# Linear attention in a fused block: chunks of 128 tokens become chunks of 64, two side by side on the partitions

## The reference, cut to what matters

```python
Q, K, V = xn @ WQ.T + bQ, xn @ WK.T + bK, xn @ WV.T + bV      # 16 heads of 64
gate = silu(xn @ Wg.T + bg)
alpha = sigmoid(alpha_logit)                                  # one decay per head and state row
def step(h, qkv):                                             # scanned over the 2048 tokens
    q, k, v = qkv
    h = alpha[None, :, :, None] * h + k[:, :, :, None] * v[:, :, None, :]
    return h, einsum('bhi,bhij->bhj', q, h)
y = (o * gate) @ WO.T + bO
x = layernorm(x + residual + y)
x = layernorm(x + coupling_network(x))
```

## Time and profile before

| | |
|---|---|
| three runs | 1981.52, 1983.5, 1986.42 us; median 1983.5 |
| the profiled execution | 1980.89 us, of which the span is 1979.2 us |
| PE busy | 1853.6 us, 94% |
| PE weight loads | 1409.0 us, 71% |
| DVE, ACT, POOL busy | 1087.8, 749.1, 315.3 us (55%, 38%, 16%) |
| granted clock | 0.983 of full over the span |

### The profile page before, as it was taken

One profiled execution on the slowest core, in us unless ns is written; L12 is line 12 of the kernel. 1 busy time (PEld: TensorE's weight loads), 2 busy tenths in 40 slices (PEclk: granted clock), 3 DMA queues, 4 the chain that ended last, 5 costly groups with the idle time before them and its releaser, 6 DMA issues.

```text
span 1979.2 us, 46951 instructions
## 1 busy us (share of the span) xinstructions
PE 1853.6 (94%) x19178; PEld 1409.0 (71%) x19178; DVE 1087.8 (55%) x2230; ACT 749.1 (38%) x1326; POOL 315.3 (16%) x246
## 2 busy tenths in 40 slices
PE   5999999999799999999889999999979999999996
PEld 4888787853587878784368787878338888888732
DVE  7646464545754655554665555555375554545546
ACT  3424242434342424334443333333444333334344
POOL 3111111101211111210221212021022121111002
PEclk9999999999899999999989999999999999999998
DMA  4000000000100000000010000000001000000001
GB/s 153 2 13 2 12 2 12 2 1 1 54 2 13 2 12 2 12 2 0 0 55 2 13 2 13 2 13 1 0 19 37 2 13 2 12 2 13 1 0 43
DMA packets 23342, 26.86 MB, mean 14 GB/s; under 512 B 3185, under 2 KB 22001, under 8 KB 23153
## 3 DMA queue, kind: packets, MB, share of 16 engines
q1 hardware_dynamic: 21152, 19.62, 3.1%
q10 hardware_dynamic: 2000, 4.20, 0.6%
HBM read 15.42 MB, written 8.39 MB: 12 GB/s over the span
## 4 chain that ended last, share of the span: by engine, by line
PE 83%; DVE 7%; issue 6%; ACT 4%; DMA 0%; POOL 0%; DVEq 0%; ACTq 0%; SPq 0%
PE bank L803 37%; PE bank L875 11%; PE bank L1029 7%; PE bank L830 6%; PE bank L866 6%; PE bank L857 5%; PE bank L847 3%; PE bank L839 2%; DVE v_sb L771 2%; DVE x_nf L764 2%; PE bank L1072 1%; DVE cpl L760 1%; PE bank L794 1%; ACT q_sb L415 1%; PE bank L1046 1%
## 5 line engine op out<-in xcount | busy, mean ns | idle before, releaser
L415 ACT ACTIVATE q_sb<-q_sb,pows 128x384 f32<-128x384 f32 (+2 forms) x387 | 168.7, 498 | 469.4 <-DVE q_sb L599 469.4
L721 DVE TENSOR_TENSOR o_g<-bank,gate 128x512 f32<-128x512 f32 x128 | 88.6, 692 | 443.1 <-PE bank L866 443.1
L345 POOL TENSOR_TENSOR k_end<-k_sc,pows 128x512 f32<-128x512 f32 x129 | 135.8, 1053 | 833.8 <-DVE k_sc L590 833.8
L433 ACT ACTIVATE h_bd<-h_seq,pows 64x256 f32<-64x256 f32 x256 | 130.0, 508 | 313.9 <-DVE h_seq L699 310.6
L875 PE MATMUL bank<-wo,o_g 128*128 128x256 f32 x1024 | 226.2, 379 | 0.0
L875 PEld LDWEIGHTS bank<-wo,o_g 128*128 128x128 f32 x1024 | 193.2, 190 | 26.2
L683 DVE COPY_PREDICATED att<-causal,bank 128x1024 f32<-128x1024 int32 x128 | 167.8, 1311 | 8.2 <-PE bank L830 8.2
L675 DVE TENSOR_TENSOR v_sb<-bank,bias_v 128x512 f32<-128x512 f32 x128 | 88.3, 692 | 103.8 <-PE bank L803 101.3
L857 PEld LDWEIGHTS bank<-q_sb,h_bd 128*128 128x128 f32 x1024 | 134.0, 191 | 11.3
L866 PE MATMUL bank<-att,v_sb 128*64 128x128 f32 x2048 | 140.1, 279 | 0.0
L830 PE MATMUL bank<-q_sb,k_sc 64*32 64x128 f32 (+3 forms) x8192 | 137.0, 237 | 0.0
(11 more groups left out here) (137 smaller groups left out, 3365.3 us busy)
## 6 DMA issues: line engine op xcount, KB each, us to landing
x_in<-in_x SPq DMA_DIRECT2D x17, 512.0 KB, 3.5
out_y<-o_g SPq DMA_DIRECT2D x16, 512.0 KB, 2.9
v_sb<-in_wq ACTq DMA_DIRECT2D x1, 1024.0 KB, 5.2
v_sb<-in_wk SPq DMA_DIRECT2D x1, 1024.0 KB, 8.3
o_g<-in_wg ACTq DMA_DIRECT2D x1, 1024.0 KB, 10.6
o_g<-in_wv ACTq DMA_DIRECT2D x1, 1024.0 KB, 13.4
wo<-in_wo ACTq DMA_DIRECT2D x1, 1024.0 KB, 17.1
bias_v<-in_bV SPq DMA_DIRECT2D x1, 512.0 KB, 9.7
```

What stands on the lines that cost most here:

```text
L345: nc.gpsimd.tensor_tensor(k_end[:].rearrange("p (a z) (b r) -> p a (z b) r", z=2, r=BL), k_sc[:].rearrange("p (a z) (b r) -> p a (z b) r", ...
L415: last = nc.scalar.activation(q_sb[:, p % 2, d].rearrange("p (a z) n -> p a (z n)", z=2)[:, :, reach], q_sb[:, p % 2, 0].rearrange("p (a z ...
L433: nc.scalar.activation(h_bd[rows, :, e * DH:(e + 1) * DH], h_seq[rows, :, :], ACT.Copy, scale=pows[rows, p, HP:HP + 1]).then_inc(s_hbd, 1)
```

## The change

The change makes chunks of `SC` = 64 tokens. The 128 partitions of a token group now hold two chunks, `r` = 0 and 1, on partitions 0 to 63 and 64 to 127; there are 8 chunks (`NSC`) in a stage in place of 4.

- `from_state`: 16 products on 64x64 places (head `e` uses rows 64e.. and columns 64e..) with 64 columns, from a plain `h_dec`, in place of 4 products of 128x128 with 128 columns from the block-diagonal `h_bd`. The output goes to banks 5 and 6, one per `r`.
- `from_chunk`: 16 products on 64x64 places with 64 columns, in place of 8 on 128x64 with 128 columns.
- `updates`: 16 products on 64x64 places in place of 8 on 128x64, 64 columns each. They go to the upper halves of banks 2 and 3, whose lower halves have the scores.
- `scores`: still 32 products per pair, but of 2 and 1 query blocks (64 and 32 columns).
- DVE: 8 dependent state steps instead of 4; they wait for scores and update both. `masked` covers 512 elements per partition in place of 1024, always behind the steps. The copy of `h_st` moves from DVE to POOL. The gating reads two banks.
- ACT: one shifted query copy instead of three, and one decay of 128x512 instead of two of 64x256.
- PE waits for its own `from_state` before `from_chunk`. In the last pair, the second `y_part` goes behind `from_state`.
- The start makes seven fewer table entries of decay powers and clears no `h_bd`.

The diff, cut to its core:

```diff
+R = 2
+SC = C // R
+SB = SC // BL
+NSC = NC * R
...
+        def update_of(c, r, rows):
+            return bank[2 + r][rows, NC * SC + c * DH:NC * SC + (c + 1) * DH]
...
@@ gpsimd
+            def state_carried(b, p, n):
+                pool.wait_ge(s_h0, b + 1)
+                pool.wait_ge(s_hend, n + C0)
+                pool.wait_ge(s_hdec, n + C0)
+                pool.sem_inc(s_passed_pool, 1)
+                nc.gpsimd.tensor_copy(h_seq[:, 0, :], h_st[:, p, :]).then_inc(s_hs, 1)
...
                     for p in range(NP - 1):
+                        state_carried(b, p, it * NP + p)
                         ends_of(p + 1, it * NP + p + 1)
...
@@ scalar
-                for d in range(1, NB):
+                for d in range(1, SB):
...
-                for e in range(2):
-                    rows = slice(e * DH, (e + 1) * DH)
-                    nc.scalar.activation(h_bd[rows, :, e * DH:(e + 1) * DH], h_seq[rows, :, :],
-                                         ACT.Copy, scale=pows[rows, p, HP:HP + 1]).then_inc(s_hbd, 1)
+                nc.scalar.activation(h_dec[:], h_seq[:], ACT.Copy, scale=pows[:, p, HP:HP + 1]).then_inc(s_hdec, 1)
...
@@ vector
-                        dve.wait_ge(s_hbd, n * 2 + C0)
-                        nc.vector.tensor_copy(h_seq[:, 0, :], h_st[:, p, :]).then_inc(s_hs, 1)
                         dve.wait_ge(s_upd, n + 1 + C0)
-                        for c in range(NC):
-                            dve.wait_ge(s_hs, n * NC + c + 1 + C0)
+                        dve.wait_ge(s_score, n + 1 + C0)
+                        for j in range(NSC):
+                            dve.wait_ge(s_hs, n * NSC + j + 1 + C0)
...
@@ tensor, scores
                 for c in range(NC):
-                    for g in range(NB):
-                        count = g + 1 if c % 2 else NB - g
+                    for g in ((1, 3, 0, 2) if c % 2 else (0, 2, 1, 3)):
+                        chunk, place = g // SB, g % SB
+                        count = place + 1 if c % 2 else SB - place
...
@@ tensor, updates
                 for c in range(NC):
-                    for e in range(2):
-                        h = 2 * p + e
-                        last = nc.tensor.matmul(
-                            bank[6][e * DH:(e + 1) * DH, c * DH:(c + 1) * DH],
-                            k_tok[:, c, e * DH:(e + 1) * DH], v_sb[:, c, h * DH:(h + 1) * DH],
-                            start=True, stop=True)
+                    for r in range(R):
+                        tok = slice(r * SC, (r + 1) * SC)
+                        for e in range(2):
+                            h = 2 * p + e
+                            last = nc.tensor.matmul(
+                                update_of(c, r, slice(e * DH, (e + 1) * DH)),
+                                k_tok[tok, c, e * DH:(e + 1) * DH], v_sb[tok, c, h * DH:(h + 1) * DH],
+                                start=True, stop=True)
...
@@ tensor, from_state
+                for r in range(R):
+                    for c in range(NC):
+                        for e in range(2):
+                            rows = slice(e * DH, (e + 1) * DH)
+                            last = nc.tensor.matmul(
+                                bank[5 + r][rows, c * SC:(c + 1) * SC], h_dec[rows, c * R + r, :],
+                                query_blocks(rows, p, c, r * SB, SB),
+                                start=(c == 0), stop=False, skip_group_check=True)
...
@@ tensor, the pair's ring
-                        pe.wait_ge(s_hbd, (n + 1) * 2 + C0)
+                        pe.wait_ge(s_hdec, n + 1 + C0)
                         pe.wait_ge(s_og, n + C0)
-                        from_state(p)
+                        pe.sem_inc(s_passed_pe, 1)
+                        from_state(p).then_inc(s_fs, 1)
...
                         pe.wait_ge(s_att, n + 1 + C0)
+                        pe.wait_ge(s_fs, n + 1)
+                        pe.sem_inc(s_passed_pe, 1)
                         from_chunk(p).then_inc(s_o, 1)
                         if p + 1 < NP:
                             pe.wait_ge(s_ktok, n + 2 + C0)
                             pe.wait_ge(s_hend, n + 1 + C0)
+                            pe.wait_ge(s_att, n + 1 + C0)
+                            pe.sem_inc(s_passed_pe, 1)
                             updates(p + 1).then_inc(s_upd, 1)
```

More of the change, by code:

```diff
@@ L127, in build, with query_blocks @@
         bank = [psum[:, n, :] for n in range(8)]
-        def query_blocks(rows, p, c, first, count):
+        def query_blocks(rows, p, c, place, count):
             view = q_sb[rows, p % 2]
-            step = -(NC * C) + BL if c % 2 else NC * C + BL
+            plane = NC * C
+            step, shifted = (BL - plane, count - 1) if c % 2 else (BL + plane, 0)
+            first = shifted * plane + c * C + place * BL
             return bass.AP(view.tensor, view.offset + first, [list(view.ap[0]), [step, count], [1, BL]])
+        def update_of(c, r, rows):
+            return bank[2 + r][rows, NC * SC + c * DH:NC * SC + (c + 1) * DH]
         def part(n, k):
@@ L830, in scores @@
                             last = nc.tensor.matmul(
[L831 to L833 removed]
+                                bank[2 + e][g * BL:(g + 1) * BL, cols], k_sc[rows, c, g * BL:(g + 1) * BL],
+                                query_blocks(rows, p, c, chunk * SB + first, count), start=True, stop=True)
                 return last
@@ L851, in updates @@
                 return last
             def from_state(p):
-                for c in range(NC):
-                    first = (NB - 1) * NC * C + c * C if c % 2 else c * C
-                    nc.tensor.matmul(bank[5][:, c * C:(c + 1) * C], h_bd[:, c, :],
-                                     query_blocks(slice(0, P), p, c, first, NB),
-                                     start=(c == 0), stop=False, skip_group_check=True)
+                for r in range(R):
[6 more added lines that the diff above has]
+                                start=(c == 0), stop=False, skip_group_check=True)
```

133 lines of the change are left out of this document (66 added, 67 removed).

## The result

The changed kernel takes 2022.1 us (median of 4 runs, 2018.5 to 2025.9), the kernel before 1982.7 (4 runs, 1981.5 to 1986.4): a ratio of 1.0196 [1.0177, 1.0215]. That it is slower is clear; whether by a little more or a little less than 2% is not. I had said 1977, range 1942 to 2016. The profiled execution has a span of 2016.8 us against 1979.2 before: 37.6 us to explain. First the page of the changed kernel, for the earlier trace rows: busy times, the queue that brings the program, the chain.

The account below looks back on a forecast made before the run. PE, busy 94% of the span, was taken to bound the kernel. Rings +1, last pairs -3, first pairs' scores -2 and start -1.5 made -5.5 us: 1980.9 to 1975.4, stated as 1977 for the median, range 1942 to 2016.

Parts of the forecast that it names:

- the sum of a ring: PE from one `from_state` to the next, 8.20 us before: 0.26 - 0.12 + 0 - 0.13 = +0.01 us, x112 = +1 us.
- The supply of products is the bound: Rival, chance 0.17: update and scores on PE cost 0.031 us a product, ring +0.27 us, total 2007 or 2010 us.
- `from_state`, +0.26: PE's state products: 16 rounds of 0.059 us plus tile-shape changes in and out, 1.15 us against 0.89.
- Transposes to update, -0.12: PE from key transposes to update: `from_chunk` halves to 0.47 us, but waiting for `k_tok` leaves only -0.12 us per pair.
- Update, 0: PE's update products: again 8 rounds, so no change from 0.56 us; bounds -0.05 and +0.15.
- Scores, -0.13: PE's 32 score products per pair: first half scales with columns to 0.19 us, second nearly stays; 0.87 against 1.00.
- Last pair, -0.18: Last pair of each stage, no update behind it, gets all of `from_chunk`'s gain: 1.83 us against 2.01, x16 = -3 us.
- DVE becomes the bound: Rival, chance 0.16: DVE's chain of steps, mask and keys reaches 8.45 us, making PE wait; total 2005 or 2007 us.
- What is hidden: DVE's chain from scores to next keys takes 7.97 us against PE's 8.21, so its four more steps cost nothing, 0.24 spare.
- Start, -1.5: Kernel start: dropping 7 table steps of 0.20 us each saves 1.5 us.
- the first pairs' scores, -0.13: Scores of each stage's first pair, outside the ring: -0.13 us x 16 = -2 us.
- the floor of 25 ns a record: Skill's start-to-start minimum for small matmuls on PE; by it the ring would be 0.3 us more; trace's 16 ns preferred.

Follow-up runs that it names:

- the shifts of the program: Changed kernel with 64 extra semaphore increments a stage in PE's program, 1999.6 us; the same with 16 increments a stage, 2006.4 us.
- the block-diagonal run: Changed kernel with `from_state` back to 8 full-array products of 64 columns from block-diagonal states: 2145.5 us, ratio 1.0813 to the kernel before.

## Why the prediction was wrong

The step that failed is the sum of a ring and its "there are 112 such rings": it takes the small products' rounds as all that their number costs. Nothing in it asks whether the instructions themselves come in time. What the runs showed in its place: PE stops about once a stage in the scores until a packet of its program is there, 19.2 us in all, and longer at each stage's head, 11.6 us with the slow clock behind it.

- **What was missing.** The stops in the scores, 19.2 us, and the longer and slower stage starts, 34.8 - 27.3 = 7.5 of stop at the jump and 4.1 behind it. Together they are 31 of the 43 us by which the sum was short (the profiled execution took 2018.5, the sum says 1975.4); the other 12 are the parts below. The first is shown by the shifts of the program and by the packets. The second is a stop that ends with a packet as well, 27.3 / 15 = 1.8 us on the mean before and 34.8 / 15 = 2.3 now, and 0.36 of the 0.50 is the packet's own time; why that is longer stays open. The rival "The supply of products is the bound" comes nearest by its name and its 2010, but not by its mechanism: it put 0.031 us on each product, and here the ordinary scores go at 0.74 / 32 = 0.023 a product. Its bound (scores and update over 1.6) isn't met in six rings of seven: they take 1.36.
- **`from_state`, +0.26.** 1.08 and the way in, which lies in the projections' 0.09: +0.28. Right; the ways in and out were both priced, and a round is 0.058 in the trace for 0.059. Full-array products would not have been cheaper, as the block-diagonal run shows.
- **Transposes to update, -0.12.** Measured 70.38 - 68.94 = 1.44 against 1.46: -0.02. PE does wait for `k_tok`, as said, but `k_tok` starts 0.70 behind the transposes, not 0.64, since those now start with a change of shape; and the update starts 0.14 behind its end, not 0.05. The later start is 0.06 of the error of 0.10, and the 0.14 is the other 0.04, since I had given 0.05 and 0.05 more for the added waits. The second pair has it too (153.57 + 0.59 to 154.30). There the record of the added increment stands at 154.19, between the end of `k_tok` and the first product, while in the kernel before the weight load itself waits and no increment lies between.
- **Update, 0.** 0.62 against 0.56, the same 0.62 that `from_chunk` takes where nothing makes it wait; within the bounds.
- **Scores, -0.13.** 0.74 against 1.00: -0.26. Two things were off. The term's parts, 0.19 and the rest of 1.00 less 0.05, give 0.83 and not 0.87. And the halves behaved the other way round. The changed kernel, first half and second:

```profile
71.00:71.26 0.26, 0.26 (x32) 0.26 (x33) 1.00 0.00 0
71.26:71.74 0.48, 0.48 (x58) 0.44 (x33) 1.00 0.00 0
```

  The first half, which I scaled to 0.19, went from 0.31 to 0.26 only; the second, which I kept at 0.64, went from 0.69 to 0.48. So neither "scales with the columns" (0.60 in all) nor a fixed price of 0.031 a product holds, and the term came out between them.
- **Ring.** +0.28 - 0.02 + 0.06 - 0.26 = +0.06, where I had +0.01. The parts' errors nearly cancel, which is luck and no proof of the terms; the ring is 0.05 x 112 = 6 us of the error.
- **Last pair, -0.18.** Measured 0.01, so 3 us of the error. The change splits the output projection in two around `from_state`; its halves take 6.14 + 6.24 against 12.09, and that takes all that `from_chunk` gives (14.08 against 14.09 in all, with `from_state`). I had priced the products and not the pieces they are put between. The second part's end with `from_chunk`:

```profile
115.76 4.91 PE L894 MATMUL bank<-wo,o_g 128*128 128x256 f32 x22
120.60 0.69 PE L885 MATMUL bank<-att,v_sb 64*64 64x64 f32 x32
...
121.23 0.50 PE L814 MATMUL bank<-x_hi,wq_hi 128*128 128x512 f32 x1
```

- **"DVE becomes the bound".** Refuted as a rival, and "What is hidden" was right: 0.19 to spare where 0.24 was forecast; a step is (74.28 - 72.06) / 7 = 0.32, the mask 0.75 less its overlap, the copy on POOL 0.24 for 0.2.
- **Start, -1.5, and the first pairs' scores, -0.13.** The first stage's first V product starts at 30.81, before at 30.38: nothing was gained at the start, 2 us of the error. A first pair's scores take 0.95 for 1.00, 1 us of it.
- **An aside.** At the floor of 25 ns a record that the prediction weighs, the 64 records of the scores would take 1.60, so the ring would be some 1.0 us longer by it and not 0.3. The choice of the row over the floor was right.

The hundredths were worked out while two questions were not asked of the profile before: how near PE's stream of instructions was to running dry, and what a PE standing still at the jump costs in clock. The first could have been read: `issue` was 6% of the chain, and the stretch that now holds 256 instructions in 2.2 us held 192 in 2.5.

## What to carry to other kernels

Count instructions as well as rounds: where a change cuts products into smaller ones, look for the stretches in which the most of them are through in the least time (here 256 in 2 to 4 us), and for "issue" in the middle of a group with a packet of the program's queue landing 1.2 to 1.6 us before its end. Such a stop hangs on where in the program it falls, so a harmless shift (a few increments where the engine has slack) tells it from a cost of the change in one run, and a variant must not be judged before that. A wait that many rings share (here `k_tok`) can be covered by exchanging two neighbours on the waiting engine, where it can't be shortened; here that took 0.23 us off each ring.

## What the hardware showed that I had not expected

- PE's program arrives in packets of 16.4 KB, and PE stops at places that lie multiples of 256 instructions apart (1474, 2242, 3009), for up to 2.4 us. All 191 such stops of over 0.7 us in six kernels end 1.2 to 1.6 us after a packet has landed. In the changed kernel PE got through the 256 before the stop in about 2.3 us, in the one with the full-array state once in 9.9. With 16 instructions of the 256 exchanged for slower ones the stop was gone or down to 0.2. A packet takes some 0.9 to 1.5 us to land in the rings; what decides when it starts stays open.
- Records of f32 products on places of 64x64 and 64x32 with few columns follow one another every 0.012 us (64 records of the scores in 0.74) to 0.019 (32 of the update in 0.62).
- A load of 128 columns of f32 weights goes at 0.108 to 0.111 us a record, whether 64 or 128 columns stream behind it.
- Increments on PE stand 0.151 us apart. 13 of them between two projections hold PE by 0.38 us in one kernel and by less in another; the 8 behind a value group cost nothing that the kernel before shows.
- After a stop of 1.8 to 2.9 us at the loop's jump the granted clock is 0.57 on the mean of some 4 us in some stages and 1.00 in others, worth 1.5 us a time.
